# Delta stage of a three-stage decoder layer: pair of batches outside, head groups inside

## The chip, the cores and the metric

The kernel runs on one core of one Trainium2 chip. The metric is the device time of one execution in microseconds (us). Everything is float32.

## The reference

Input x is 8 batches of 256 tokens of width 512. One decoder layer with three parts is computed, and after each part a residual sum and a layer norm over the width (written here with `ln`):

```
x = ln(x + gated_delta_attention(x))   # the stage of this change
x = ln(x + cross_attention(x))         # 32 heads of 16, with a mask
x = ln(x + selected_token_block(x))    # a router picks 1 token of 8, these go through attention and an MLP
```

The first part, per head of 128, with 8 query and key heads and 16 value heads:

```
q, k, v = silu(causal_conv4(x @ w_qkv.T));  q, k = l2_norm(q), l2_norm(k)
beta = sigmoid(x @ w_beta.T);  alpha = exp(-exp(log_A) * softplus(x @ w_alpha.T + dt_bias))
for each token t:                      # S is a 128 x 128 state per value head
    S = S * alpha[t];  u = (v[t] - k[t] @ S) * beta[t];  S = S + outer(k[t], u);  o[t] = q[t] @ S
y = (silu(x @ w_gate.T) * rms_norm(o)) @ w_out.T
```

## The kernel before

`delta_phase` (line 62) does the first part, `cross_phase` (983) the second and `ffn_phase` (1564) the third. Each is a block of five programs, one an engine, written out in full with semaphores between them. The change touches `delta_phase` alone.

The unit of work there is a double: one group of heads (one query and key head with its two value heads; GH = 8 groups) for one pair of batches (2 x 256 = 512 tokens; PAIRS_B = 4 pairs). There are 32 doubles. They are worked through in a software pipeline of slots. Slot w projects double w + 1 (its six products with 128 columns of weights each: query, key, two values, two gates), solves double w (the recurrence within a chunk of 128 tokens, by repeated small products), and finishes double w - 1 (state, output, rms norm, gate, output projection and the sum into `tokens`). `slots` (line 883) calls one function for each engine with w from -1 to 32. Slot -1 only projects, slot 31 has no projection, and slot 32 only finishes double 31.

In the kernel before, double w is group w // 4 and pair w % 4, so four doubles in a row share their weights.

On PE (`pe_slot`, 189) all products of a slot stand in one fixed order: `products`, `turn_tokens`, `post_w0`, then `proj(0)` to `proj(5)` cut in pieces, between which stand the solving steps `f_step(1..4)` and `g_step(1..4)` (64 products of 32 x 32 each), `f32`, `g32`, `f64`, `g64`, and the steps of `post`. `proj(m)` (193) waits for its 128 columns of weights (`w_loaded[m]`), and for the bank that it writes. `post_out` (372) waits for `w_out_loaded` and for `gated_made`.

DVE (`dve_slot`, 625) does the three later taps of the convolution, the scans that make the decays (`scan`, 639), the masks and joins between f and g steps, and the sum into `tokens` (`add`, 679). ACT does the first tap, the activations and some copies out of PSUM. POOL prepares `dec_gam`, `first` and `kq_p`.

SP issues all DMAs of the stage in one queue (lines 890 to 934), in this order: x and the first weights, constants, then, for w from 0 to 31: `rows(w)` (912), three transfers that bring the alphas of double w from a DRAM buffer, spread over all partitions (762 KB; it waits for both scans of double w - 1); at w = 0 also all of `tokens` (4 MB) and four tables; where w is a multiple of 4, six loads of 256 KB into `w_g`, each after the projection m of the double before has read its part (`projected`); and where w % 4 is 1, the 512 KB of `wo_g`, after the last `y_done` of the group before. After the loop come four loads of 1 MB into `x_t`, weights of the second part.

Weights are single-buffered: `w_g` is [128, 4, 6, 128] and `wo_g` is [128, 2, 512].

`decays_from_logits` (684) computes all alphas of all doubles in slot -1. Its last step (718) multiplies by `neg_a` for the two value heads in two instructions. The column order of beta and alpha is that of the doubles (`unit_cols`, 174).

The layer norm of the first part needs all 8 groups of a pair to be added. `average` and `normalise` (727, 735) do it on DVE and `measure` (514) on ACT, for pairs 0, 1 and 2 in slots 30, 31 and 32 (`finished`, 755). That of pair 3 is done at the start of `cross_phase`.

Of the kernel before, what the change touches and what calls it, by code (L numbers as in the profile page):

```python
# [61 lines left out]
def delta_phase(nc, sem_stack, tokens, x_t, ident, sources, alpha_dram, ahead):  # L62

    w_in, conv_w, w_out = sources["w_in"], sources["conv_w"], sources["w_out"]
    with ExitStack() as stack:
# [108 lines left out]
        def unit_cols(tile, c, j):  # L174

            return tile.rearrange("p (g i h j c) -> p i h g j c", g=GH, i=4, h=2, j=VH)[:, :, :, :, j, c]
# [12 lines left out]
        def pe_slot(pe, w, project, solve, post):  # L189
            par, oth, nxt = w % 2, (w + 1) % 2, w + 1  # L190
            batch, group = nxt % PAIRS_B, nxt // PAIRS_B

            def proj(m, k0, k1):
                bank = bank_p[m % 2]
                if k0 == 0:
                    pe.wait_ge(w_loaded[m], 16 * (group + 1))
                    if m < 2:
                        wait(pe, gate_ready, 2 * nxt - 1 + m)
                    else:
                        wait(pe, conv_step, 12 * nxt + 3 * (m - 1))  # L200
                for k in range(k0, k1):
                    mm = pe.matmul(bank[:, :], w_g[:, k, m, :], x_t[:, k, 2 * S * batch:2 * S * (batch + 1)],  # L202
                                   start=(k == 0), stop=(k == KC - 1))
                if k1 == KC:
                    mm.then_inc(projected, 1)
# [166 lines left out]
            def post_out(n):  # L372
                e, c = divmod(n, NC)
                if n == 0:
                    wait(pe, w_out_loaded, 16 * ((w - 1) // PAIRS_B + 1))
                if n < 2:
                    wait(pe, gated_made, 2 * (w - 1) + n + 1)
                for j in range(VH):
                    mm = pe.matmul(y_banks[n][:, :], gated[:, e, j, c * P:(c + 1) * P], wo_g[:, j, :],  # L379
                                   start=(j == 0), stop=(j == VH - 1))  # L380
                mm.then_inc(y_done, 1)
# [106 lines left out]
        def act_slot(act, w, project, solve, post):  # L488
            par, oth, nxt = w % 2, (w + 1) % 2, w + 1
            group = nxt // PAIRS_B  # L490
# [114 lines left out]
            if w - 2 >= DOUBLES - PAIRS_B:  # L605
                measure(w - 2 - DOUBLES + PAIRS_B)
# [18 lines left out]
        def dve_slot(v, w, project, solve, post):  # L625
            par, oth, nxt = w % 2, (w + 1) % 2, w + 1
            group = nxt // PAIRS_B
# [51 lines left out]
            def add(n):  # L679
                at = tokens[:, 4 * ((w - 1) % PAIRS_B) + n, :]  # L680
                wait(v, y_done, 4 * (w - 1) + n + 1)
                v.tensor_tensor(at, at, y_banks[n][:, :], ALU.add).then_inc(y_added, 1)  # L682

            def decays_from_logits():
# [33 lines left out]
                for j in range(VH):  # L718
                    op = v.tensor_tensor(
                        log_alpha.rearrange("p (g b j c) -> p g b j c", g=GH, b=B, j=VH)[:, :, :, j, :],  # L720
                        poly.rearrange("p (g b j c) -> p g b j c", g=GH, b=B, j=VH)[:, :, :, j, :],
                        neg_a[:].rearrange("p (g j o) -> p g j o", j=VH, o=1)[:, :, j:j + 1, :].to_broadcast([P, GH, B, NC]), ALU.mult)
# [32 lines left out]
            finished = w - 2 - DOUBLES + PAIRS_B  # L755
# [132 lines left out]
        with nc.Block() as block:  # L888

            @block.sync  # L890
            def _(sp):
# [26 lines left out]

                for w in range(DOUBLES):
# [5 lines left out]
                    if w and w % PAIRS_B == 0:  # L925
                        for m in range(6):
                            wait(sp, projected, 6 * (w - 1) + m + 1)
                            sp.dma_start(w_g[:, :, m, :], w_in[w // PAIRS_B][:, :, m * P:(m + 1) * P]).then_inc(w_loaded[m], 16)
                    if w % PAIRS_B == 1:
                        wait(sp, y_done, 4 * (w - 1))  # L930
                        sp.dma_start(wo_g[:], w_out[w // PAIRS_B]).then_inc(w_out_loaded, 16)
                sp.wait_ge(projected, 6 * DOUBLES)
                for to, source in ahead[1]:
                    sp.dma_start(to, source).then_inc(ahead[2], 16)

# [1180 lines left out]
```

## Time and profile before

| | us |
|---|---|
| three runs | 2861.43, 2856.67, 2858.89 |
| median | 2858.89 |
| the profiled execution | 2858.66 |
| its span, first to last instruction | 2856.9 |

The page of the profile has busy times of each engine, the span in 40 slices, the DMA queues, the chain that ended last and the costliest groups of instructions. The chain of the page covers only the end of the last stage (from 2629 us on), which says little of the delta stage. In what follows a slot is told by its first `products` matmul (line 228): slot 0 starts at 50.48 us of the span, slot 1 at 91.41, slot 2 at 141.56, slot 6 at 341.78, slot 7 at 393.07, slot 14 at 743.43, slot 22 at 1145.07, slot 30 at 1548.96 and slot 31 at 1599.01; the second part starts at 1673.10.

### The profile page before, as it was taken

The numbers are of one execution on the slowest core, as the hardware profiler recorded it, in microseconds if no ns is written. First come the engines' busy times: TensorE is split into PE (matmuls) and PEld (weight loads), VectorE is DVE, ScalarE is ACT, GpSimd is POOL, SyncE is SP. The second block draws the span as 40 slices with busy tenths as digits, with TensorE's granted clock in tenths as the row PEclk, the third lists the DMA queues.
The fourth block names the chain that finished last, engine by engine and source line by source line (L and its number), as shares of the span: only waits on it lengthen the run. The fifth ranks groups of instructions, "written<-read, shape, count | busy, mean of one in ns | idle before, by whom it ended". The sixth has DMA issues, their size and how long they took to land. (4 is left out here: it accounts for less than half of the span.)

```text
span 2856.9 us, 80959 instructions
## 1 busy us (share of the span) xinstructions
PE 2723.1 (95%) x34198; PEld 1688.1 (59%) x34198; DVE 1829.7 (64%) x5116; ACT 1315.4 (46%) x3201; POOL 548.5 (19%) x690
## 2 busy tenths in 40 slices
PE   6999999999999999999999889999999999986998
PEld 3565655656555565555656556666666666653466
DVE  5565555556556555565656537888888988886533
ACT  3343343434334343343434226666766676774131
POOL 1222212122221222222122132132131221200020
PEclk9999999999999999999999889999999999998999
DMA  5010110110101101101101100000000000001341
GB/s 186 23 36 12 31 46 20 31 29 20 43 17 32 35 13 31 35 13 31 46 2 32 61 31 1 13 7 7 13 1 13 13 2 13 2 1 62 144 185 67
DMA packets 96777, 99.97 MB, mean 35 GB/s; under 512 B 38177, under 2 KB 84385, under 8 KB 95265
## 3 DMA queue, kind: packets, MB, share of 16 engines
q1 hardware_dynamic: 96256, 94.27, 10.3%
q8 instruction: 272, 4.46, 0.7%
q14 instruction: 89, 0.72, 0.1%
q0 software_dynamic: 160, 0.52, 0.0%
HBM read 89.93 MB, written 4.85 MB: 33 GB/s over the span
## 5 line engine op out<-in xcount | busy, mean ns | idle before, releaser
L202 PE MATMUL dr_p<-x_t,dr_w_g 128*128 128x512 f32 x1536 | 742.0, 610 | 11.0 <-DMA dr_w_g<-in_w_in 7.6
L1259 ACT ACTIVATE xa_probs<-xa_probs,xa_low 128x256 f32<-128x256 f32 x1024 | 430.2, 497 | 18.2 <-DVE xa_low L1426 13.8
L202 PEld LDWEIGHTS dr_p<-x_t,dr_w_g 128*128 128x128 f32 x1536 | 268.9, 191 | 227.8 <-issue 217.6
L1191 PEld LDWEIGHTS xa_t<-ident,xa_probs 128*128 128x128 f32 x2048 | 224.6, 141 | 159.3 <-ACT xa_probs L1259 97.8
L1191 PE MATMUL xa_t<-ident,xa_probs 128*128 128x128 f32 x2048 | 286.0, 280 | 21.8 <-ACT xa_probs_t L1265 15.3
L636 DVE SCALAR_TENSOR_TENSOR dr_acc<-dr_p,dr_taps,dr_acc 128x510 f32<-128x510 f32 (+2 forms) x384 | 285.2, 743 | 23.4 <-ACT dr_acc L494 15.5
L1426 DVE CUSTOM_DVE_ANT_0 xa_probs<-xa_s,xa_mask 128x256 f32<-128x256 f32 x512 | 209.6, 409 | 77.5 <-PE xa_s L1178 77.5
L1265 ACT ACTIVATE xa_probs_t<-xa_t 128x512 f32<-128x512 f32 x256 | 152.5, 596 | 230.2 <-PE xa_t L1191 230.2
L1426 DVE CUSTOM_DVE_ANT_0 xa_probs<-xa_s,xa_zeros 128x256 f32<-128x256 f32 x512 | 214.6, 419 | 0.0
L1435 DVE COPY xa_probs_t<-xa_t 128x512 f32<-128x512 f32 x256 | 176.4, 689 | 41.6 <-PE xa_t L1191 30.4
L854 POOL TENSOR_TENSOR dr_first<-dr_n_mat,dr_packed 32x256 f32<-32x256 f32 x128 | 92.1, 719 | 505.1 <-DVE dr_n_mat L762 499.5
L494 ACT ACTIVATE dr_acc<-dr_p,dr_taps 128x512 f32<-128x512 f32 x128 | 87.3, 682 | 181.4 <-PE dr_p L202 181.4
L1178 PE MATMUL xa_s<-xa_keys,xa_q_pair 32*128 32x512 f32 x1024 | 156.2, 651 | 1.7 <-DVE xa_low L1426 1.0
L1206 PEld LDWEIGHTS xa_o<-xa_probs_t,xa_val 128*32 128x32 f32 x4096 | 105.4, 110 | 83.0 <-issue 76.6
L1206 PE MATMUL xa_o<-xa_probs_t,xa_val 128*32 128x128 f32 x4096 | 139.7, 277 | 14.4 <-DVE xa_probs_t L1435 12.8
L868 POOL COPY dr_x_half<-dr_yx 32x256 f32<-32x256 f32 x32 | 12.4, 387 | 729.1 <-DVE dr_yx L677 729.1
L265 PEld LDWEIGHTS dr_g<-dr_yx,dr_f_low 32*32 32x32 f32 x8192 | 83.2, 105 | 110.9 <-issue 63.1
L682 DVE TENSOR_TENSOR tokens<-tokens,dr_m 128x512 f32<-128x512 f32 x64 | 44.0, 688 | 137.8 <-PE dr_m L379 137.8
L379 PE MATMUL dr_m<-dr_wo_g,dr_gated 128*128 128x512 f32 x256 | 126.9, 620 | 0.4 <-DVE dr_gated L832 0.4
L265 PE MATMUL dr_g<-dr_yx,dr_f_low 32*32 32x32 f32 x8192 | 97.8, 195 | 24.1 <-DVE dr_f_low L669 20.5
L255 PEld LDWEIGHTS dr_f<-dr_yx,dr_n_mat 32*32 32x32 f32 x8192 | 82.7, 105 | 64.3 <-DVE dr_yx L770 28.7
L1552 POOL TENSOR_TENSOR xa_by_sin<-xa_raw,sin 128x256 f32<-128x256 f32 x64 | 45.0, 724 | 387.6 <-DVE xa_raw L1303 387.6
(308 smaller groups left out, 4741.3 us busy)
## 6 DMA issues: line engine op xcount, KB each, us to landing
dr_alpha<-alpha_rows SPq DMA_DIRECT2D x64, 254.0 KB
dr_w_g<-in_w_in SPq DMA_DIRECT2D x48, 256.0 KB, 6.0
dr_alpha<-alpha_rows SPq DMA_DIRECT2D x32, 256.0 KB
ff_wide<-in_fw_qkv SPq DMA_DIRECT2D x8, 1024.0 KB, 15.3
x_t<-in_x_t SPq DMA_DIRECT2D x4, 1024.0 KB, 7.3
tokens<-in_x_tok SPq DMA_DIRECT2D x1, 4096.0 KB, 15.7
dr_wo_g<-in_w_out SPq DMA_DIRECT2D x8, 512.0 KB, 3.7
xa_ctx_b<-in_ctx_t SPq DMA_DIRECT2D x8, 512.0 KB, 3.9
```

Of the source, the lines that this page charges most:

```text
L202: mm = pe.matmul(bank[:, :], w_g[:, k, m, :], x_t[:, k, 2 * S * batch:2 * S * (batch + 1)], start=(k == 0), stop=(k == KC - 1))
L265: mm = pe.matmul(bank_g[i, n * TR:(n + 1) * TR], f_low[i, n, :], yx[i, 0, n, :], start=True, stop=True)
L379: mm = pe.matmul(y_banks[n][:, :], gated[:, e, j, c * P:(c + 1) * P], wo_g[:, j, :], start=(j == 0), stop=(j == VH - 1))
L636: v.scalar_tensor_tensor(out=to[:, :, d:S], in0=bank[:, :, 0:S - d], scalar=taps[:, group, m, TAPS - 1 - d:TAPS - d], in1=to[:, :, d:S], o ...
L854: op = g.tensor_tensor(first[i], n_mat[i, :, i], packed[i, LOW:LOW + 1, :].to_broadcast([TR, EA, TR]), ALU.mult)
L1178: pe.matmul(bank_s[i][:, :], q_pair[32 * i:32 * i + 32, par, t, h, q * P:(q + 1) * P], keys[32 * i:32 * i + 32, par, t].rearrange("p k n - ...
L1191: mm = pe.transpose(bank_t[i % 2][:, at:at + P], probs[:, v % 3, i, kind, kt * P:(kt + 1) * P], ident)
L1206: mm = pe.matmul(bank_o[32 * i:32 * i + 32, at:at + P], val[:, par, kind, kt, 4 * t + i, h:h + 2], probs_t[:, v % 2, i, kind, kt, :], star ...
L1259: op = act.activation(at, at, ACT.Exp, bias=low[:, v % 3, i, kind:kind + 1], scale=-1.0)
L1265: act.activation(probs_t[:, v % 2, 2 * m].rearrange("p k t n -> p (k t n)"), bank_t[0][:, :], ACT.Copy)\
L1426: op = dve.tensor_tensor_reduce(out=probs[:, v % 3, i, kind, :], in0=bank_s[i][:, kind * S:(kind + 1) * S], in1=mask[:, par, q, :] if kind ...
L1435: dve.tensor_copy(probs_t[:, v % 2, 2 * m + 1].rearrange("p k t n -> p (k t n)"), bank_t[1][:, :]).then_inc(copied[1], 1)
```

## The change

The doubles are put in another order: double w is now pair w // 8 and group w % 8. All eight groups of a pair of batches follow each other, and then comes the next pair. Four things go with it.

- Each slot needs weights of another group, so SP loads the six parts of `w_g` for every w from 1 to 31 and `wo_g` for every double. The load of `wo_g` for double w - 2 is issued behind the `w_g` loads of w, and the last two stand behind the loop, the first of them ahead of the four 1 MB loads of the second part and the other behind these.
- The columns of beta and alpha take the new order, and the product with `neg_a` is cut in eight instructions where there were two.
- The layer norm of pairs 0, 1 and 2 is done in slots 9, 17 and 25.
- Indices and the values of waits follow.

```diff
@@ -173,7 +173,7 @@
 
         def unit_cols(tile, c, j):
 
-            return tile.rearrange("p (g i h j c) -> p i h g j c", g=GH, i=4, h=2, j=VH)[:, :, :, :, j, c]
+            return tile.rearrange("p (i g h j c) -> p i h g j c", g=GH, i=4, h=2, j=VH)[:, :, :, :, j, c]
 
         EA = 2 * VH * NC
         BLOCK = [slice(TR * i, TR * i + TR) for i in range(4)]
@@ -188,12 +188,12 @@
 
         def pe_slot(pe, w, project, solve, post):
             par, oth, nxt = w % 2, (w + 1) % 2, w + 1
-            batch, group = nxt % PAIRS_B, nxt // PAIRS_B
+            batch = nxt // GH
 
             def proj(m, k0, k1):
                 bank = bank_p[m % 2]
                 if k0 == 0:
-                    pe.wait_ge(w_loaded[m], 16 * (group + 1))
+                    pe.wait_ge(w_loaded[m], 16 * (nxt + 1))
                     if m < 2:
                         wait(pe, gate_ready, 2 * nxt - 1 + m)
                     else:
@@ -372,7 +372,7 @@
             def post_out(n):
                 e, c = divmod(n, NC)
                 if n == 0:
-                    wait(pe, w_out_loaded, 16 * ((w - 1) // PAIRS_B + 1))
+                    wait(pe, w_out_loaded, 16 * w)
                 if n < 2:
                     wait(pe, gated_made, 2 * (w - 1) + n + 1)
                 for j in range(VH):
@@ -487,7 +487,7 @@
 
         def act_slot(act, w, project, solve, post):
             par, oth, nxt = w % 2, (w + 1) % 2, w + 1
-            group = nxt // PAIRS_B
+            group = nxt % GH
 
             def tap(m):
                 wait(act, projected, 6 * nxt + m + 1)
@@ -602,8 +602,8 @@
             if post:
                 wait(act, den_made, w)
                 act.activation(rms_den[:], rms_den[:], ACT.Sqrt).then_inc(rooted, 1)
-            if w - 2 >= DOUBLES - PAIRS_B:
-                measure(w - 2 - DOUBLES + PAIRS_B)
+            if w > GH and w % GH == 1:
+                measure(w // GH - 1)
             if project:
                 silu_v(0)
                 tap(3)
@@ -624,7 +624,7 @@
 
         def dve_slot(v, w, project, solve, post):
             par, oth, nxt = w % 2, (w + 1) % 2, w + 1
-            group = nxt // PAIRS_B
+            group = nxt % GH
 
             def conv(m, first=1, end=TAPS):
                 wait(v, tapped, 4 * nxt + m + 1)
@@ -677,7 +677,7 @@
                 v.transpose(yx[:, 1].rearrange("p n k -> p (n k)"), at).then_inc(yx_done, 1)
 
             def add(n):
-                at = tokens[:, 4 * ((w - 1) % PAIRS_B) + n, :]
+                at = tokens[:, 4 * ((w - 1) // GH) + n, :]
                 wait(v, y_done, 4 * (w - 1) + n + 1)
                 v.tensor_tensor(at, at, y_banks[n][:, :], ALU.add).then_inc(y_added, 1)
 
@@ -715,11 +715,12 @@
                 then(v.tensor_tensor(poly, poly, small, ALU.add))
                 then(v.tensor_tensor(poly, poly, big, ALU.add))
                 v.wait_ge(expa_made, 1)
-                for j in range(VH):
-                    op = v.tensor_tensor(
-                        log_alpha.rearrange("p (g b j c) -> p g b j c", g=GH, b=B, j=VH)[:, :, :, j, :],
-                        poly.rearrange("p (g b j c) -> p g b j c", g=GH, b=B, j=VH)[:, :, :, j, :],
-                        neg_a[:].rearrange("p (g j o) -> p g j o", j=VH, o=1)[:, :, j:j + 1, :].to_broadcast([P, GH, B, NC]), ALU.mult)
+                of_pair = lambda x, i, j: x.rearrange("p (i g b j c) -> p i g b j c", i=4, g=GH, b=2, j=VH)[:, i, :, :, j, :]
+                for i in range(4):
+                    for j in range(VH):
+                        op = v.tensor_tensor(of_pair(log_alpha, i, j), of_pair(poly, i, j),
+                                             neg_a[:].rearrange("p (g j o) -> p g j o", j=VH, o=1)[:, :, j:j + 1, :].to_broadcast([P, GH, 2, NC]),
+                                             ALU.mult)
                 op.then_inc(arg_made, 1)
                 v.wait_ge(alpha_turned, 1)
                 v.tensor_copy(alpha_rows, bank_f[:, 0:2 * P].rearrange("p (a m) -> p a m", a=2)).then_inc(rows_made, 1)
@@ -752,7 +753,7 @@
                 scan(0)
                 scan(1)
                 return
-            finished = w - 2 - DOUBLES + PAIRS_B
+            finished = w // GH - 1 if w % GH == 1 else -1
             if solve:
                 wait(v, kq_done, w + 1)
                 wait(v, dec_gam_made, w + 1)
@@ -916,22 +917,27 @@
                     for at, c, skip in ((1, 0, 1), (P + 1, 1, 1), (S + 1, 1, 0)):
                         sp.dma_start(to[:, :, at:at + P - skip], source[c][:, skip:P].partition_broadcast(P)).then_inc(alpha_loaded, 16)
 
+                def out_weights(w):
+                    wait(sp, y_done, 4 * w)
+                    sp.dma_start(wo_g[:], w_out[w % GH]).then_inc(w_out_loaded, 16)
+
                 for w in range(DOUBLES):
                     rows(w)
                     if w == 0:
                         sp.dma_start(tokens[:], sources["x_tok"]).then_inc(tokens_loaded, 16)
                         for to, source in ahead[0]:
                             sp.dma_start(to, source).then_inc(ahead[2], 16)
-                    if w and w % PAIRS_B == 0:
+                    if w:
                         for m in range(6):
                             wait(sp, projected, 6 * (w - 1) + m + 1)
-                            sp.dma_start(w_g[:, :, m, :], w_in[w // PAIRS_B][:, :, m * P:(m + 1) * P]).then_inc(w_loaded[m], 16)
-                    if w % PAIRS_B == 1:
-                        wait(sp, y_done, 4 * (w - 1))
-                        sp.dma_start(wo_g[:], w_out[w // PAIRS_B]).then_inc(w_out_loaded, 16)
+                            sp.dma_start(w_g[:, :, m, :], w_in[w % GH][:, :, m * P:(m + 1) * P]).then_inc(w_loaded[m], 16)
+                    if w > 1:
+                        out_weights(w - 2)
+                out_weights(DOUBLES - 2)
                 sp.wait_ge(projected, 6 * DOUBLES)
                 for to, source in ahead[1]:
                     sp.dma_start(to, source).then_inc(ahead[2], 16)
+                out_weights(DOUBLES - 1)
 
             @block.tensor
             def _(pe):
```

## Rows read from the trace of the kernel before

**Rows 1.** The page: busy us of each engine; packets and MB of q8.

```profile
PE 2723.1 (95%) x34198; PEld 1688.1 (59%) x34198; DVE 1829.7 (64%) x5116; ACT 1315.4 (46%) x3201; POOL 548.5 (19%) x690
...
q8 instruction: 272, 4.46, 0.7%
```

**Rows 2.** Sums by slot: us, busy of PE, PEld, DVE, ACT, POOL; PE clock, DMA share.

```profile
50.48:91.41 40.93, 37.11 (x702) 19.92 (x700) 22.66 (x41) 13.25 (x22) 12.30 (x17) 0.96 0.32 107
191.63:241.68 50.05, 49.43 (x777) 29.60 (x776) 28.91 (x51) 19.52 (x52) 10.27 (x15) 1.00 0.07 18
341.78:393.07 51.29, 49.63 (x777) 29.69 (x776) 28.90 (x51) 19.52 (x52) 10.27 (x15) 1.00 0.17 48
...
944.87:994.92 50.05, 49.43 (x777) 29.60 (x776) 28.91 (x51) 19.52 (x52) 10.27 (x15) 1.00 0.18 50
1145.07:1198.57 53.50, 51.39 (x778) 30.35 (x777) 28.91 (x51) 19.51 (x52) 10.27 (x15) 0.97 0.16 46
1548.96:1599.01 50.05, 49.43 (x777) 29.60 (x776) 33.54 (x64) 19.71 (x53) 10.27 (x15) 1.00 0.14 55
1599.01:1673.10 74.09, 56.40 (x795) 40.51 (x793) 33.02 (x70) 17.52 (x71) 8.22 (x13) 0.75 0.06 22
```

**Rows 3.** PE at g_step(3), slots 6 and 22; stops of L265; sums of a stretch.

```profile
373.92 0.37 PE L265 MATMUL dr_g<-dr_yx,dr_f_low 32*32 32x32 f32 x19 [1.03 <-issue]
...
1177.52 0.57 PE L265 MATMUL dr_g<-dr_yx,dr_f_low 32*32 32x32 f32 x43 [1.48 <-issue]
...
  issue: 3.6, 3
...
1178.20:1181.60 3.40, 3.40 (x5) 1.34 (x6) 2.89 (x6) 0.23 (x1) 2.20 (x6) 0.51 0.02 5
```

**Rows 4.** DMA queues in 366.5 to 371.2, 371.2 to 372.5, 418.57 to 420.67.

```profile
q1 hardware_dynamic: 2032, 1.01, 76.8%
...
q8 instruction: 1, 0.02, 5.7%
...
q8 instruction: 1, 0.02, 2.8%
```

**Rows 5.** SP's queue in slot 6.

```profile
364.41 2.08 SPq L928 DMA_DIRECT2D dr_w_g<-in_w_in  x3
```

**Rows 6.** DMA issues: count, KB each, median us to landing.

```profile
dr_w_g<-in_w_in SPq DMA_DIRECT2D x48, 256.0 KB, 6.0
tokens<-in_x_tok SPq DMA_DIRECT2D x1, 4096.0 KB, 15.7
```

**Rows 7.** Start of slot 0: DVE, SP, PE, and the landing of wo_g.

```profile
35.87 0.49 DVE L719 TENSOR_TENSOR dr_junk<-dr_junk,dr_neg_a 128x128 f32<-128x128 f32 x2
47.42 3.42 DVE L642 TENSOR_TENSOR_SCAN dr_decay<-dr_alpha,dr_scan_in 128x770 f32<-128x770 f32 x2 [1.92 <-DMA dr_alpha<-alpha_rows]
...
50.87 3.92 SPq L917 DMA_DIRECT2D dr_alpha<-alpha_rows  x3
54.83 2.41 SPq L931 DMA_DIRECT2D dr_wo_g<-in_w_out  x1
...
53.29 4.46 PE L202 MATMUL dr_p<-x_t,dr_w_g 128*128 128x512 f32 x10
58.90 0.75 PE L255 MATMUL dr_f<-dr_yx,dr_n_mat 32*32 32x32 f32 x64 [1.15 <-DVE dr_yx L770]
...
DMA to landing us min/median/max: 7.2/7.2/7.2
```

**Rows 8.** DVE in slots 31 and 32: layer norm, mask(3), add(0).

```profile
1615.92 2.43 DVE L729 BATCH_NORM_STATS2 dr_stats<-tokens 128x6 f32<-128x512 f32 x4
1619.27 0.42 DVE L669 TENSOR_TENSOR dr_f_low<-dr_f,dr_packed 128x256 f32<-128x256 f32 x1 [0.51 <-PE dr_f L255]
...
1663.85 1.91 DVE L741 TENSOR_SCALAR tokens<-tokens,dr_moments,dr_ln_den 128x512 f32<-128x512 f32 x4
1666.76 0.69 DVE L682 TENSOR_TENSOR tokens<-tokens,dr_m 128x512 f32<-128x512 f32 x1 [1.00 <-PE dr_m L379]
```

## The prediction

> **What bounds the kernel now.** I read the page first, then the sums by slot, then the PE instructions of single slots, then the DMA queues. The page [rows 1] shows PE busy for 95% of the span, so time comes only from what makes PE wait. The delta stage runs from 50.48 us (first products of slot 0) to 1673.10, and the sums by slot [rows 2] are nearly constant: a slot takes 50.05 us with 49.43 of PE in it, whether it carries no weights (191.63) or a reload of 1.5 MB (944.87, DMA share 0.18). Of the seven slots that reload weights (2, 6, 10, ... 26) four take 50.05 to 50.07. Two (6 and 14) take 51.29 and one, slot 22, takes 53.50. The last two slots, 31 and 32, have no projection and leave PE gaps.
>
> The three long slots are the clue. In slot 6, PE stops inside the burst of 64 small matmuls of g_step(3), 19 before their end, for 1.03 us, released by "issue", which is by nothing the profile knows [rows 3]. In slot 22 it stops 43 before the end, for 1.48 us. Over the kernel this line has exactly 3 such stops [rows 3]; slot 14 has the third. PE's program is unrolled and comes by a DMA queue of its own, in 272 packets (q8) [rows 1], so one packet per some 250 of its matmuls and weight loads, six a slot. In slot 6 no q8 packet runs from 366.5 to 371.2 us, while the main queue is 77% busy with 2032 packets; the one that PE needs comes after, in 371.2 to 372.5 [rows 4]. PE resumes at 373.92. I read this as an instruction fetch that waited behind the three alpha transfers and the first three weight loads, the latter issued at 22.6 to 24.7 us of the slot [rows 5].
>
> **The change part by part.** The sum is made against the profiled execution's 2858.66 us (span 2856.9), which is 0.23 below the median 2858.89.
>
> *Reordering alone.* The same 32 doubles with the same matmuls are done; PE's instruction count stays, so a fetch falls on the same instruction of each slot as before. Index changes cost 0.
>
> *Steady weight loads.* SP now loads six chunks of w_g in each of slots 0 to 29 and 512 KB of wo_g at each slot's end: 24 x 1.5 + 24 x 0.5 = 48 MB more. A chunk is overwritten when its projection ends and is used a slot (50 us) later; its landing takes 6.0 us [rows 6], and wo_g, loaded at a slot's end for the end of the next, took 7.2 in its slowest place [rows 7], so the weights themselves are on time, by some 40 us. SP waits for projected and y_done, and behind it are only the alpha rows of the next double, which wait for a scan in the middle of the next slot: nothing late. Volume: 2.75 MB a slot against 50 us, at a DMA share of 0.18 as in the reload slots. Cost 0 for data, and 0 is what four of seven reload slots show.
>
> *Fetch stalls in new places.* A quiet slot stalls once it has weights if its fetch is asked for while the burst is queued and is needed in g_step(3), at about 30.9 us of the slot. In quiet slots such a fetch shows itself between 25.5 and 27.6 us: the queue view of that stretch has a q8 packet (slot 7 [rows 4]) or none. I read this stretch for slots 1 to 29: 14 quiet ones have it (1, 4, 5, 7, 12, 13, 15, 19, 20, 21, 23, 27, 28, 29), none of the seven reload slots has it, but the three that stall are those whose fetch came after it. In 4, 12 and 19 the block boundary lies behind the burst by my count of instructions, so these do not stall. In 1 and 23 the fetch is asked for while the burst is still being issued, so I count them half. That is 14 - 3 - 1 = 10 stalls, each at 51.29 - 50.05 = 1.24 us: 12.4 us. Bounds: 0 (four of seven) and 14 x 3.45 = 48.3 if all were as slot 22. I take 12.4, since rows of two equal slots give it.
>
> *Clock.* After the stall of slot 22 PE was granted 0.51 (1.2 GHz) from 1178.20 to 1181.60 [rows 3]; that slot cost 3.45, so 2.2 more than the others. One of three stalls did so. PE had stood for 0.62 and 1.48 us just before. With stalls mostly of 1.03, I take 3 of the 10 new ones: 6.6 us. Bounds 0 and 10 x 2.2 = 22.
>
> The Trainium skill ("Runtime: NRT & Kernel Launch", Instruction fetch mechanics) says that each engine's program is refilled in blocks of 16 KiB by a DMA queue that the sequencer drives, and that this is mostly hidden. The trace agrees with the block size (q8: 272 packets, 4.46 MB) and, in three slots, not with "hidden". A second rule speaks against my reading: "DMA: Bandwidth & Descriptors" (Queues, rings and completion order) says that a DMA engine takes turns between its queues packet by packet, so a fetch would not wait for a queue to drain. Rows 4 disagree. By that rule the two terms above would be 0.
>
> *Slot 0.* Before, slot 0 projects double 1 with weights already there: PE runs proj(0) from 53.29 for 4.46 us, then f_step(1) at 58.90 [rows 7]. Now proj(0) waits for w_g[0] of the next group, which SP issues behind rows(1), which waits for both scans (47.42 to 50.84). SP's three alpha issues take 50.87 to 54.79, because 4 MB of tokens (issued 41.40, 15.7 us to landing [rows 6]) are ahead of them. In this place SP issued wo_g at 54.83 and it landed 7.2 us later, 62.0 [rows 7]. w_g[0] has half its bytes, so I estimate 60.3. The eight small products with neg_a that replace two (0.49 us [rows 7]) cost 0.7 more on the chain to the alpha rows: bounds 0.2 and 8 x 0.245 - 0.49 = 1.5. So proj(0) starts at 61.0, f_step(1) 4.46 later at 65.5, 6.6 us late. The first chunk is not the last wait: w_g[1] follows within some 1.9 us, under the 3.4 us of proj(0). PE, idle for 7.7 us, probably gets the lower clock for a while: 3.4 us at 0.51 cost 1.7; I take 1.4. Together 8.0. Bounds: 5 (load lands with the tokens, no clock loss) and 13 (chunks 1.9 us apart make each projection wait).
>
> *Layer norm of finished pairs.* It moves from slots 30, 31, 32 to 9, 17, 25: 2.43 for the statistics and 1.91 for the normalising [rows 8], some 4.9 us of DVE each with the small steps between. Slot 30 with it took 50.05 as slots without it [rows 2], so 0 in the new places. In slot 31 the statistics end before mask(3), which waits 0.51 us for PE all the same; the normalising delays f_64 (1632.78) by under 1 us, but PE is at post_out(0) from 1631.75 for 3.78. In slot 32 it ends at 1665.76 and add(0) waits 1.00 for PE. Gain 0; bounds 0 and 2 x 4.9 = 9.8.
>
> *Tail.* The 4 MB of cross weights, issued at 1591.07 and landing up to 11 us later, now go behind wo_g of slot 31, at about 1600. They are needed at 1673, but PE's fetch in slot 31, which ran at about 1607.7, would wait until 1612: 0 to 4 us, I take 1.5. The last wo_g is issued at about 1642 and needed at 1663.2: hidden.
>
> Sum: 12.4 + 6.6 + 8.0 + 1.5 = 28.5; 2858.66 + 28.5 = 2887.2.
>
> **The rivals.**
> A: fetches are not held by weight traffic, or only in the phases seen, since the stops of slots 6, 14 and 22 have another cause. For it: four of seven reload slots are clean. Against it: no quiet slot has any such stop. Time: 2858.66 + 8.0 = 2867. (The Trainium skill's rule of queues taking turns, told above, would bring it out this way.)
> B: most stalls take the clock with them and the tail stalls in full: 10 x 3.45 + 2 x 1.24 + 8 + 4 = 49, so 2908. For it: slot 22. Against: slots 6 and 14.
> C: faster. The layer norm on DVE in the drain slots 31 and 32 is what sets mask(3) and the adds; taken away it gives up to 9.8 us, and fetch stalls and slot 0 cost nothing: 2849. It decides from the point where DVE, not PE, ends those waits; the 0.51 and 1.00 us of [rows 8] ended by PE speak against it.
> D: no change. Weights are in time also in slot 0 (the queue drains faster without wo_g there) and fetches as in A: 2859 to 2864. Against it: SP can't issue before 54.8.
>
> **How the numbers follow.** Forecast 0.62, A 0.17, B 0.10, C 0.04, D 0.07. A change under 0.2% (5.7 us) can't be told from none in this kernel. Slower: 0.62 + 0.17 + 0.10 = 0.89, minus 0.01 for a short A: 0.88. Same: D and that 0.01: 0.08. Faster: 0.04. The range takes in A and most of B: 2865 to 2906. The forecast's own terms reach from 2872 (five stalls, no clock) to 2902.
>
> **What would show it.** (1) Slot 0, from its first products to the next, 40.9 us before, is 48 to 50, PE stops before L202 for w_g, 7 to 8 us. (2) L265 has some 13 stops by "issue" in place of 3, each 1 to 1.5 us, in slots 5, 7, 8, 13, 15, 20, 21, 27, 28, 29 and the old ones; slots without them stay at 50.05. (3) The granted clock dips three to four more times between 100 and 1550 us. (4) Slots 9, 17, 25 don't grow by the layer norm, and slots 31 and 32 together stay at 74.1 plus up to 4. If no slot stalls but 6, 14 and 22, the fetch step is wrong; if PE waits for dr_w_g in steady slots, the step on data is.

## The result and the profile after

The changed kernel takes 2881.09 us (median of 6 runs, 2878.95 to 2887.01), the kernel before 2858.28 beside it (6 runs, 2856.67 to 2861.55). The ratio is 1.0084, 95% interval 1.0071 to 1.0096: slower by 22.8 us. The forecast was 2887.2. The profiled execution took 2881.02 us, with a span of 2879.0.

From the page after: busy us and share of the span by engine, the DMA queues, two groups of PE (busy, mean ns | idle before them and its main releaser), and the weight loads with the median us to landing.

```profile
PE 2730.6 (95%) x34198; PEld 1691.2 (59%) x34198; DVE 1829.9 (64%) x5122; ACT 1316.1 (46%) x3201; POOL 548.8 (19%) x690
...
q1 hardware_dynamic: 175744, 144.61, 16.6%
q8 instruction: 272, 4.46, 0.7%
...
L202 PE MATMUL dr_p<-x_t,dr_w_g 128*128 128x512 f32 x1536 | 749.5, 615 | 18.1 <-DMA dr_w_g<-in_w_in 14.8
...
L265 PE MATMUL dr_g<-dr_yx,dr_f_low 32*32 32x32 f32 x8192 | 100.0, 194 | 32.5 <-DVE dr_f_low L669 20.5
...
dr_w_g<-in_w_in SPq DMA_DIRECT2D x192, 256.0 KB, 5.6
```

PE issues the same number of instructions and the same 272 blocks of program as in [rows 1]. The loads of w_g are 192 instead of 48 and land no later than in [rows 6] (median 5.6 us against 6.0). Slots start at other times than before, so the sums are taken from the first `products` of each slot (us; busy of PE, PEld, DVE, ACT, POOL; PE clock, DMA share, GB/s). These are slots 0, 5, 6, 7, 8, 9, 15 and 22, slots 31 and 32 together, and the stretch of low clock in slot 7:

```profile
52.02:100.45 48.43, 38.70 (x701) 20.55 (x700) 22.31 (x40) 13.26 (x22) 10.64 (x16) 0.89 0.44 126
301.65:352.26 50.61, 49.70 (x777) 29.76 (x776) 28.91 (x51) 19.54 (x52) 10.27 (x15) 1.00 0.21 59
352.26:403.40 51.14, 49.63 (x778) 29.68 (x777) 28.91 (x51) 19.54 (x52) 10.28 (x15) 1.00 0.21 58
403.40:456.91 53.51, 51.39 (x778) 30.33 (x777) 28.91 (x51) 19.54 (x52) 10.27 (x15) 0.97 0.23 56
456.91:508.98 52.07, 49.65 (x778) 29.71 (x777) 28.91 (x51) 19.54 (x52) 10.27 (x15) 1.00 0.23 57
508.98:559.03 50.05, 49.42 (x778) 29.60 (x777) 33.52 (x64) 19.74 (x53) 10.26 (x15) 1.00 0.22 60
810.37:863.19 52.82, 51.30 (x778) 30.26 (x777) 28.90 (x51) 19.55 (x52) 10.25 (x15) 0.97 0.22 57
1164.81:1217.92 53.11, 51.32 (x778) 30.12 (x777) 28.92 (x51) 19.54 (x52) 10.29 (x15) 0.97 0.20 56
1620.86:1696.28 75.42, 55.94 (x795) 39.93 (x794) 23.51 (x44) 17.18 (x69) 8.22 (x14) 0.77 0.18 71
436.90:440.31 3.41, 3.41 (x6) 1.35 (x4) 2.54 (x6) 0.00 (x0) 2.44 (x7) 0.50 0.03 5
```

Slots 2 to 4, 9 to 12, 16 to 19, 23 to 26 and 30 take 50.04 to 50.08 us, as the quiet slots of [rows 2] did; slot 9 does so with 4.6 us more of DVE work, the layer norm. The others are longer; those not shown, 1, 13, 14, 20, 21, 27, 28 and 29 take 51.03, 50.53, 50.68, 50.74, 50.67, 50.88, 50.51 and 51.30. The 14 longer slots carry 18.9 us over 50.05, against 5.9 before.

PE's own order in time, in slots 0, 8 and 31 (start, us, count, idle before and its releaser), and the sum of PE's idle time at L265 between 100 and 1615 us, which is slots 1 to 30:

```profile
62.06 7.61 PE L202 MATMUL dr_p<-x_t,dr_w_g 128*128 128x512 f32 x10 [7.06 <-DMA dr_w_g<-in_w_in]
...
487.42 0.31 PE L265 MATMUL dr_g<-dr_yx,dr_f_low 32*32 32x32 f32 x10 [0.62 <-DVE dr_f_low L669]
489.52 0.67 PE L265 MATMUL dr_g<-dr_yx,dr_f_low 32*32 32x32 f32 x54 [1.80 <-issue]
...
1634.73 0.72 PE L255 MATMUL dr_f<-dr_yx,dr_n_mat 32*32 32x32 f32 x60 [1.11 <-issue]
...
1638.48 0.25 PE L265 MATMUL dr_g<-dr_yx,dr_f_low 32*32 32x32 f32 x4 [1.30 <-issue]
```

```profile
its engine sat idle before it (us, times) until:
...
  issue: 10.7, 14
```

There are 14 stops by "issue" where [rows 3] have 3; a fifteenth stop of this line is the one of 1.30 us in slot 31. In slot 8 the burst of 64 is cut after 10; in the other slots the cut lies elsewhere in the same 64.

SP's queue in slots 0 and 8, and the DMA queues in slot 8 (the second fence: from 482.0 to 486.8, and then from 486.8 to 488.2):

```profile
50.23 4.69 SPq L918 DMA_DIRECT2D dr_alpha<-alpha_rows  x3
54.97 6.93 SPq L933 DMA_DIRECT2D dr_w_g<-in_w_in  x6
...
478.03 1.47 SPq L918 DMA_DIRECT2D dr_alpha<-alpha_rows  x3
479.54 7.82 SPq L933 DMA_DIRECT2D dr_w_g<-in_w_in  x4
```

```profile
q1 hardware_dynamic: 2042, 1.01, 87.6%
...
q1 hardware_dynamic: 47, 0.02, 6.9%
q8 instruction: 1, 0.02, 5.0%
```

For 4.8 us no program block comes in while 2042 packets of the main queue do. When these are through, the block arrives (486.8 to 488.2), and PE goes on at 489.52. This is the picture of [rows 4], now in a slot that was quiet before.

### The profile page after: what moved, and what is told of

The parts are those of the page before. It is cut to its first block and busy times, and to the rows that moved or that the text cites. A ratio compares the mean times of both kernels' runs of the same rounds, so it can differ in the third digit from the quotient of the medians.

```text
span 2879.0 us, 81133 instructions
## 1 busy us (share of the span) xinstructions
PE 2730.6 (95%) x34198; PEld 1691.2 (59%) x34198; DVE 1829.9 (64%) x5122; ACT 1316.1 (46%) x3201; POOL 548.8 (19%) x690
## 3 DMA queue, kind: packets, MB, share of 16 engines
q8 instruction: 272, 4.46, 0.7%
## 5 line engine op out<-in xcount | busy, mean ns | idle before, releaser
L202 PE MATMUL dr_p<-x_t,dr_w_g 128*128 128x512 f32 x1536 | 749.5, 615 | 18.1 <-DMA dr_w_g<-in_w_in 14.8
L202 PEld LDWEIGHTS dr_p<-x_t,dr_w_g 128*128 128x128 f32 x1536 | 271.2, 193 | 239.8 <-issue 222.3
L869 POOL COPY dr_x_half<-dr_yx 32x256 f32<-32x256 f32 x32 | 12.4, 387 | 748.1 <-DVE dr_yx L677 748.1
L265 PEld LDWEIGHTS dr_g<-dr_yx,dr_f_low 32*32 32x32 f32 x8192 | 84.1, 105 | 120.6 <-issue 72.1
L265 PE MATMUL dr_g<-dr_yx,dr_f_low 32*32 32x32 f32 x8192 | 100.0, 194 | 32.5 <-DVE dr_f_low L669 20.5
L255 PEld LDWEIGHTS dr_f<-dr_yx,dr_n_mat 32*32 32x32 f32 x8192 | 82.6, 105 | 64.3 <-issue 29.9
```

The source lines that it names most:

```text
L265: mm = pe.matmul(bank_g[i, n * TR:(n + 1) * TR], f_low[i, n, :], yx[i, 0, n, :], start=True, stop=True)
```

## The experiments

The prediction's theory, "order of arrival": a block of PE's program stands behind all data packets issued before it, and PE stops where it runs out of program. No view shows when a block is asked for. The time used here is an estimate: PE passes the place one block (256 of its records) ahead of the stop at 24.6 to 24.9 us of the slot in 11 of the 14 stopping slots, and at 26.1 to 27.3 in slots 5, 20 and 27. Rivals were that the data of the loads is late, that the new order or the layer norm costs, that the clock alone does it, and that fetches and data take turns. Each kernel is compared with the kernel before on its own chip.

**The new order alone.** Against the changed kernel the loads and their waits are the old ones, so most slots use the weights of another group.

```diff
-                    if w:
+                    if w and w % PAIRS_B == 0:
                         for m in range(6):
-                    if w > 1:
-                        out_weights(w - 2)
+                    if w % PAIRS_B == 1:
+                        wait(sp, y_done, 4 * (w - 1))
+                        sp.dma_start(wo_g[:], w_out[w // PAIRS_B]).then_inc(w_out_loaded, 16)
```

> The new order of doubles and its layer norm in slots 9, 17, 25, with weights loaded only in every fourth slot as before (so most slots use weights of another group; every instruction on the compute engines stays). My theory, that the whole cost lies in the added loads (fetches of PE's program held behind them, the first reload in slot 0, the tail): 2858 to 2860 us, stalls by issue in slots 6, 14, 22 alone, slot 0 at 40.9 us. Rival, that order or layer norm cost something of their own: above 2863. Rival, that the layer norm's leaving the drain slots gives something: below 2855.

Measured: 2857.08 us, ratio 1.0004 (0.9994 to 1.0014). Nine of the ten runs took 2854.86 to 2857.57; one took 8264.96, which nothing here explains and which is not in the ratio. Slots 0, 6 and 7, and 31 with 32:

```profile
53.37:93.73 40.36, 37.06 (x701) 19.61 (x700) 22.31 (x40) 13.25 (x22) 11.91 (x17) 0.96 0.32 104
344.17:395.44 51.27, 49.63 (x777) 29.69 (x776) 28.90 (x51) 19.52 (x52) 10.27 (x15) 1.00 0.17 48
395.44:445.50 50.06, 49.44 (x778) 29.60 (x777) 28.89 (x51) 19.52 (x52) 10.27 (x15) 1.00 0.06 18
...
1598.90:1672.29 73.39, 56.23 (x795) 40.34 (x793) 23.59 (x44) 17.15 (x69) 8.20 (x13) 0.77 0.05 22
```

PE stops at L265 in 6, 14 and 22 alone. The order, the layer norm in slots 9, 17 and 25 and the eight small products cost nothing that shows. The last two slots are 0.7 us shorter than before: the most that the layer norm can have given. Even this need not be its work, since the old order mended (below) has 73.12 us there with the layer norm where it was.

**The loads alone.** The kernel before, but w_g and wo_g loaded again in every slot, with the values that they hold already.

```diff
-                    if w and w % PAIRS_B == 0:
+                    if w:
                         for m in range(6):
-                    if w % PAIRS_B == 1:
-                        wait(sp, y_done, 4 * (w - 1))
-                        sp.dma_start(wo_g[:], w_out[w // PAIRS_B]).then_inc(w_out_loaded, 16)
+                    if w > 1:
+                        out_weights(w - 2)
```

> The old order of doubles, with its weights loaded again in every slot (the same values). My theory: the cost comes back in full, 2879 to 2883 us, with stalls by issue in slots 1, 5 to 8, 13 to 15, 20 to 22, 27 to 29, slot 0 near 48. Rival, that the cost comes from the order (which weights or alphas are read when): 2858 to 2862.

Measured: 2878.68 us, ratio 1.0083 (1.0060 to 1.0105). Slots 0 and 20:

```profile
51.50:101.53 50.03, 38.97 (x701) 20.46 (x699) 22.30 (x40) 13.26 (x22) 11.92 (x17) 0.90 0.44 133
1061.58:1114.61 53.03, 51.17 (x777) 30.37 (x776) 28.90 (x51) 19.54 (x52) 10.29 (x15) 0.97 0.20 56
```

Within the interval the loads are the whole loss, though not slot by slot: slot 0 is 1.6 us longer than in the change and slots 1 to 30 are 1.6 us shorter together. Slots 1, 5, 6, 8, 13 to 15, 20 to 22 and 27 to 29 are long; of the 14 only slot 7 is not.

**Fewer packets ahead of the fetch.** The first two loads of w_g go ahead of the alpha rows (their parts are free early in the slot), the other four stay behind.

```diff
                 for w in range(DOUBLES):
+                    if w:
+                        chunks(w, range(2))
                     rows(w)
...
                     if w:
-                        for m in range(6):
-                            wait(sp, projected, 6 * (w - 1) + m + 1)
-                            sp.dma_start(w_g[:, :, m, :], ...).then_inc(w_loaded[m], 16)
+                        chunks(w, range(2, 6))
```

> As the changed kernel, but SP issues the first two weight loads of a slot as soon as their projections end (about 7 and 14 us into the slot), ahead of the alpha rows, so the burst at 21 us of a slot has one weight load in it and not three; the bytes are the same. My theory (a fetch waits for what is queued ahead of it): the burst is drained by about 27 us of the slot, all stalls at g_step(3) vanish, also in 6, 14 and 22, and slot 0 starts a few us earlier: 2856 to 2862 us. Rival, that the stalls come from the amount of traffic in a slot and not its place: within 3 us of 2881.

Measured: 2862.79 us, ratio 1.0022 (1.0013 to 1.0032). Slots 0 and 8, and then the DMA queues of slot 8 from 473.88 to 476.70 and from there to 478.00:

```profile
53.29:98.67 45.38, 37.60 (x701) 20.24 (x699) 22.30 (x40) 13.25 (x22) 11.30 (x17) 0.92 0.48 142
449.28:499.33 50.05, 49.43 (x777) 29.61 (x776) 28.89 (x51) 19.52 (x52) 10.27 (x15) 1.00 0.21 60
```

```profile
q1 hardware_dynamic: 1069, 0.53, 82.5%
...
q1 hardware_dynamic: 163, 0.08, 21.6%
q8 instruction: 1, 0.02, 4.3%
```

The same bytes in each slot, and no stop by "issue" in any of slots 1 to 30. The block still comes after the queue has run down, but from 476.78, 27.5 us into the slot, instead of 29.9. Of the 22.8 us some 6 (by the ratio) to 8 (by the medians on this chip) are left: slot 0 has 5.1 us of wait for w_g left and the last two slots take 75.6.

**The block boundaries moved.** Some small products more in slot -1, before `sums`, shift every later PE instruction against the blocks. One such product in float32 counts as four instruction records. I had taken it for two, so the first kernel, with 64 products, shifts by 256 records (its page has PE and PEld x34326 each, where the change has x34198), a whole block, and not by half of one as its expectation says.

```diff
+                wait(pe, squared, 1)
+                for _ in range(16):          # 8 in the second kernel
+                    for n, i in enumerate(BLOCK):
+                        pe.matmul(bank_m[1][i, 0:TR], ones[:, :], qk_sq[:, n // 2, n % 2, 0:TR], start=True, stop=True)
                 sums()
```

> As the changed kernel, with 64 tiny products more in slot -1 (128 instructions of PE more, about 1 us at most), so that each fetch boundary falls 128 instructions earlier in every slot. My theory: the stalls move to the slots whose boundary now falls into the later part of g_step(3): 2, 3, 4, 9, 10, 11, 16, 17, 18, 19, 24, 25, 26 (12 perhaps), and none stays in 5, 6, 7, 8, 13, 14, 15, 20, 21, 22, 27, 28, 29; total within 6 us of 2881. Rival, that the stalling slots are set by their data or by the order of doubles: the same slots as in the changed kernel stall.

Measured: 2879.45 us, ratio 1.0082 (1.0061 to 1.0102). The stops stay in the same slots, 1, 5, 7, 8, 13 to 15, 20 to 22 and 27 to 29, with slot 6 down to 50.29 and slot 16 at 50.18. The expectation failed, and for the reason above the run tells only that the small products by themselves do nothing. With 32 products it is half a block:

> The run with 64 tiny products moved every PE instruction by 256 records, a whole block of its program, since each product is four records; so it was no shift, and the same slots stalled. Here 32 tiny products stand in slot -1, 128 records, half a block. My theory: the stalls leave 1, 5 to 8, 13 to 15, 20 to 22, 27 to 29 and come in slots 2, 3, 4, 10, 11, 17, 18, 19, 24, 25, 26, with 9, 12 and 16 at the border; the total stays within 6 us of 2881. Rival, that a stalling slot is made by its place in the order or its data: the same slots as before.

Measured: 2877.20 us, ratio 1.0073 (1.0053 to 1.0093). Slots 3, 8 and 18:

```profile
204.03:255.13 51.10, 49.58 (x778) 29.67 (x776) 28.90 (x51) 19.54 (x52) 10.29 (x15) 1.00 0.20 58
456.44:506.49 50.05, 49.43 (x778) 29.59 (x777) 28.90 (x51) 19.54 (x52) 10.29 (x15) 1.00 0.21 60
959.31:1012.29 52.98, 51.37 (x777) 30.17 (x776) 28.90 (x51) 19.54 (x52) 10.27 (x15) 0.97 0.22 56
```

The set turns over. Slots 2, 3, 4, 10, 11, 17, 18 and 24 to 26 now stop at L265, and 6 to 8, 13 to 15, 20 to 22, 28 and 29 are at 50.04 to 50.08. Slot 5, which the expectation had as quiet, stays at 50.53, but its stop (1.02 us) is now at L202; slot 16, at the border, takes 50.31. No data, no wait and no length of a product has changed in them. Counting PE's records from the first, each such stop of slots 1 to 30 falls on the same place of a block of 256 (193 or 194), and so does the one at L202 in slot 5. This holds in each of the six traces counted so (before, the change, the loads alone, the two of this section, and slot 0 alone).

**More packets, ahead and behind.** A spare transfer of 192 KB (384 packets) in each slot, once between the alpha rows and the first load of w_g, once behind the third load.

```diff
+                        wait(sp, spare_loaded, 16 * (w - 1))      # first kernel: ahead of the loop over m
+                        sp.dma_start(spare[:], w_in[w % GH][:, 0:3, 0:P]).then_inc(spare_loaded, 16)
                         for m in range(6):
                             wait(sp, projected, 6 * (w - 1) + m + 1)
                             sp.dma_start(w_g[:, :, m, :], ...).then_inc(w_loaded[m], 16)
+                            if m == 2: ...                        # second kernel: the same two lines here
```

> As the changed kernel, with one more transfer of 192 KB (384 packets) in every slot, into a tile that nobody reads, issued between the alpha rows and the first weight load. My theory, that a fetch waits for all that stands in the queues before it: about 1 us more (384 packets at some 350 in a us) in each of the 14 stalling slots, some new stalls at the borders (4, 12, 19, 23, 30), 2892 to 2905 us. Rival, that a fetch takes turns with the queue: within 3 us of 2881.

> The same 192 KB in each slot, but issued behind the third weight load, at about 25 us of the slot, which is after the critical fetch has been asked for (24.4 to 24.9). If the DMA engines serve in order of arrival, the stalls stay as they are: 2879 to 2885 us. If instead the fetch is served last, when the queue runs dry, they grow as in the run with the transfer ahead: 2892 to 2905.

Measured: 2881.25 us ahead (2875.19 and 2887.31; 1.0087, 1.0058 to 1.0116), 2883.82 behind (1.0096, 1.0076 to 1.0116). Behind came out as expected. Ahead did not: neither the median nor, in the profiled run (2875.19), the stops grew; they are 0.27 to 1.32 us there. SP's queue shows why, in slot 7 of the first kernel, which begins at 404.30:

```profile
426.96 0.51 SPq L934 DMA_DIRECT2D dr_spare<-in_w_in  x1
427.51 2.98 SPq L937 DMA_DIRECT2D dr_w_g<-in_w_in  x3
```

and of the second, beginning at 404.29:

```profile
426.94 2.04 SPq L935 DMA_DIRECT2D dr_w_g<-in_w_in  x3
429.03 2.25 SPq L938 DMA_DIRECT2D dr_spare<-in_w_in  x1
```

Ahead, SP needs until 430.49 for the third load, 26.2 us into the slot and so later than the 24.7 at which the fetch is taken to be asked for; behind, until 428.98. The spare transfer pushed a bigger one past the fetch: 1536 + 384 + 1024 = 2944 packets were ahead of it instead of 3072. That fits the theory, but it was seen only afterwards, and the two runs of each kernel lie too far apart to tell the kernels from each other by time. The run that was built on it:

**The third load behind the fourth.** The fourth waits for a projection that ends later, so this keeps exactly two loads (2560 packets) ahead of the fetch.

```diff
-                        for m in range(6):
+                        for m in (0, 1, 3, 2, 4, 5):
```

> As the changed kernel, but the third weight load is issued behind the fourth, at 30 us of the slot, so 2560 packets and not 3072 stand ahead of the critical fetch (with the extra transfer of 192 KB ahead there were 2944, since it pushed the third load behind the fetch). Arrival order: the fetch starts at 28.0 to 28.8 us of a slot, where it was 28.6 to 29.9 with three loads and 26.9 to 28.3 with one; stalls of 0 to 0.6 us in under ten slots, 2866 to 2873 us. If instead the length of the whole burst, or traffic as such, mattered, the stalls would stay: 2878 or more.

Measured: 2870.56 us, ratio 1.0053 (1.0035 to 1.0071). Slots 5 and 8:

```profile
302.16:356.27 54.11, 51.32 (x778) 30.26 (x776) 28.90 (x51) 19.54 (x52) 10.28 (x15) 0.97 0.20 55
456.77:506.81 50.04, 49.41 (x777) 29.58 (x776) 28.91 (x51) 19.54 (x52) 10.30 (x15) 1.00 0.21 60
```

The time came out as expected, and nearly all slots. Slots 5, 7, 14, 15 and 27 remain longer (54.11, 50.42, 50.64, 50.85, 50.93) and the rest are quiet: 6.8 us in all over 50.05 instead of 18.9. The miss is slot 5, which takes most of that: its block started at 30.8 and PE stopped for 2.17 us, where 28.8 and 0.6 were the most expected.

Four kernels now differ in the packets issued ahead of the fetch. In slots 5, 7, 13, 15, 21, 27 and 29, the mean time of the slot at which the block's packet starts:

| ahead of the fetch | packets | block starts, mean (range) | over 50.05, slots 1 to 30 |
|---|---|---|---|
| alpha rows (kernel before) | 1536 | 26.5 (26.0 to 27.5) | none in these slots |
| and one load (two go before the rows) | 2048 | 27.7 (26.9 to 28.3) | none |
| and two loads (third behind fourth) | 2560 | 28.6 (27.4 to 30.8) | 6.8 |
| and three loads (the change) | 3072 | 29.2 (28.7 to 29.9) | 18.9 |

Each 512 packets put the block off by 0.6 to 1.1 us. With the change PE's last program before it ends at 30.8 to 31.3, and PE resumes 2.5 to 2.8 us after the block's start (slot 8: 29.9 and 32.6), so by this estimate a start before about 28.4 costs nothing.

The traces can also say how many packets went first. In these seven slots the main queue had started 1529, 2055, 2519 and 2955 packets on the mean between 21 us of the slot and the block's start, for the four rows of the table. The two kernels with the spare transfer had 2925 (ahead) and 3107 (behind), with the block at 29.1 and 29.3. Order of arrival gives 2944 and 3072 for them; a block that waited for the whole queue would have let 3456 go first. Single slots differ (2480 to 3420 with the transfer behind).

**Slot 0 alone.** Four of the six loads for double 1 are issued in slot -1, before the alpha rows and the tokens.

```diff
+                for m in range(4):
+                    chunk(1, m)
                 sp.wait_ge(rows_made, 1)
...
-                        for m in range(6):
+                        for m in range(4 if w == 1 else 0, 6):
```

> As the changed kernel, but four of the six weight loads for double 1 are issued in slot -1, as soon as the projections of double 0 have read their parts, ahead of the alpha rows and the tokens. My theory: PE's wait of 7 us before proj(0) of slot 0 goes, slot 0 is back at 41 us, total 7 to 8 us less than 2881, about 2873; all stalls at g_step(4) stay. Rival, that another wait takes its place in slot 0 (the scans and dec_gam come later too, or the tokens behind): 2876 or more.

Measured: 2873.91 us, ratio 1.0062 (1.0045 to 1.0079). Slots 0 and 5:

```profile
53.28:91.81 38.53, 35.45 (x701) 19.42 (x699) 22.31 (x40) 13.26 (x22) 10.85 (x16) 1.00 0.43 127
292.83:346.75 53.92, 51.13 (x777) 30.33 (x776) 28.91 (x51) 19.54 (x52) 10.29 (x15) 0.97 0.20 55
```

Slot 0 has no wait for w_g and is 9.9 us shorter than in the change; the median is 7.2 lower, as the stops of the later slots stay and vary from run to run (slot 5 took 2.16 us and a stretch of low clock here).

**Both cures, in the new and in the old order.** The new order with four early loads for double 1, two loads ahead of the alpha rows later on, and the 4 MB for the second part ahead of the last two wo_g; and the kernel before with two loads ahead of the alpha rows in its seven reload slots, nothing else.

```diff
+                chunks(1, range(4))                        # new order
                 sp.wait_ge(rows_made, 1)
...
+                    if w > 1:                              # old order: if w and w % PAIRS_B == 0
+                        chunks(w, range(2))
                     rows(w)
```

> The new order with the first two weight loads of a slot ahead of the alpha rows, four weight loads of double 1 in slot -1, and the 4 MB of cross weights issued ahead of the last two loads of wo_g, as in the kernel before. My theory: no stall at g_step(4) in any slot (5.9 us of before's own three go too), slot 0 back at 41 us, tail back at 74: 2881.1 - 18.9 - 7.5 - 1.3 = 2853.4 us, ratio about 0.998 to the kernel before. Rival, that steady loads keep a small price (50.07 for 50.05 a slot, scans and fetches shifted): 2856 to 2860, no gain.

> The kernel before with one edit: in the seven slots that reload weights the first two loads are issued ahead of the alpha rows. My theory: the stalls of slots 6, 14 and 22 go, 4 to 6 us less than the kernel before: 2853 us, ratio 0.998. Rival, that they move to other instructions: no change.

Measured: the new order 2851.83 us (11 runs, 2850.20 to 2854.92), ratio 0.9983 (0.9974 to 0.9992); the old order 2852.76 (11 runs, 2851.16 to 2854.91), ratio 0.9988 (0.9979 to 0.9997); the kernel before 2856.61 (21 runs). New order, slots 0 and 5, and 31 with 32:

```profile
54.09:94.96 40.87, 37.09 (x701) 19.77 (x700) 22.31 (x40) 13.26 (x22) 12.33 (x17) 0.96 0.44 134
295.31:346.49 51.18, 49.62 (x777) 29.67 (x776) 28.91 (x51) 19.54 (x52) 10.30 (x15) 1.00 0.22 58
...
1598.02:1670.74 72.72, 55.60 (x795) 39.96 (x793) 23.61 (x44) 17.19 (x69) 8.24 (x14) 0.79 0.10 37
```

Old order, slot 6:

```profile
343.88:393.94 50.06, 49.44 (x777) 29.60 (x776) 28.91 (x51) 19.54 (x52) 10.30 (x15) 1.00 0.18 49
```

Both are faster than the kernel before by less than 0.2%, with intervals that end just below 1, and not to be told from each other (0.9 us apart, intervals overlap). The old order has no stop left in slots 6, 14 and 22. The new order has one, in slot 5, where the block started at 29.7 though only 2048 packets were ahead. The queue moved slowly there: SP's three alpha issues took 2.94 us where slot 8 has 1.47, and 1122 packets had started by 27 us of the slot where slot 8 has 1583. Why is open.

## Why the prediction was right, and what was mis-sized

The direction and the mechanism were right, and the time is 6.1 us under the forecast. By its own steps:

*Reordering, layer norm, small products: 0.* Shown by the run of the order alone (1.0004).

*Data of steady loads: 0.* Right. From slot 0 on, PE waits for w_g in slot 0 alone, and with the same bytes in another order (two loads before the rows) no later slot is longer.

*Fetch stalls, forecast 12.4.* The places were right. The ten slots named (5, 7, 8, 13, 15, 20, 21, 27, 28, 29) all stop, 4, 12 and 19 do not, and of the two counted half, 1 does and 23 does not: 11 new stops where 10 were forecast. For slot 8, which has the longest stop, this was luck: its fetch began at 24.9 us of the slot in the kernel before, ahead of the stretch that was read, so it is not among the 14 slots of the working, and the list of signs names it all the same. The size was not right. The stops by "issue" come to 10.7 us in 14, 0.76 each, from 0.26 to 1.80; the forecast took 1.24 a slot, a stop of 1.03 and what goes with it, from slots 6 and 14. Each costs some 0.2 us beyond its recorded length (slot 6: 51.14 - 50.05 - 0.89). The three old stops also became shorter (0.89, 0.47 and 1.17 us). So the step made 7.1 (10.7 - 3.6) and 2.2 (11 x 0.2), together 9.3.

*Clock, forecast 6.6.* There were three stretches at 0.50 (1.2 GHz), in slots 7, 15 and 22, where one was before: two more, not three. They cost 1.7 to 1.8 each beyond the stop (slot 7: 3.46 - 1.50 - 0.2; slot 22: 3.06 - 1.17 - 0.2), where 2.2 was taken, so 3.5. Together with the stalls this is 12.8, by which slots 1 to 30 grew (1520.4 against 1507.6); the forecast had 19.0. These two terms are the mis-sized part of the sum. Which stop takes the clock with it was not forecast well and is not explained: slot 15 lost it after a stop of 0.89, slot 8 kept it after 1.80.

*Slot 0, forecast 8.0: 7.5.* The wait for w_g was 7.06 (forecast 7 to 8), then PE ran proj(0) at 0.50, in 7.61 us instead of the 4.46 of [rows 7], 3.15 more. Against that stand the wait of 1.15 before f_step(1) and a stretch of low clock of the kernel before at 68.9, some 1.7 us, that both went. The clock's net 1.5 is near the 1.4 taken. Shown to be the loads' place by the run with early loads.

*Tail, forecast 1.5: 1.3* (75.42 against the 74.09 of [rows 2]). As the step expected, PE's fetch came behind the 4 MB: SP issued them at 1621.4 to 1623.3, and from 1622 to 1631 no block arrived while the main queue was 99% busy. PE stops by "issue" for 1.11 us at L255 and again for 1.30 us at L265. These are 2.4 us for a growth of 1.3; what gave the rest back is not shown.

*Not forecast.* Slot 0 begins 1.5 us later (52.02 against 50.48). In the kernels of this study it began between 50.5 and 55.0, 53.4 with the loads of before, so it is not put down to the change. With 12.8 over slots 1 to 30, 7.5, 1.3 and 1.5 the parts make 23.1; the profiled runs differ by 22.4, the medians by 22.8.

One name was wrong: the burst in which PE stops is that of g_step(4), not g_step(3). It has the same line and the right time of the slot, and nothing in the sum depends on it.

Of the rivals, A (no fetch stalls) falls with the moved block boundaries and with the two loads ahead of the alpha rows. B had nearly every new stop take the clock with it; 2 of 11 did. C falls with the order alone (0.7 us at most in the last two slots), D with the wait of 7.06 us in slot 0. The rule of the Trainium skill that was weighed ("DMA: Bandwidth & Descriptors", Queues, rings and completion order: a DMA engine takes turns between its queues packet by packet) would have the block come as soon without the third load as with it. The runs say otherwise: it starts later with each load ahead of it, from 26.5 to 29.2 us.

What stays open: in which part of the DMA path the block waits (the starts fit an order of arrival, but no view shows the path), and what decides the clock. Not tried: larger packets for w_g, which would change the number of packets at the same bytes; the study varied both together.

## What to carry to other kernels

In a fully unrolled kernel a DMA burst can stop an engine that needs none of its data, because its program comes by DMA too and here started later with each load issued before it (26.5 to 29.2 us of the slot): where PE stops by "issue" in the midst of equal instructions, look at the instruction queue in that stretch, and at what was issued just before it. The cure here was to move loads, not to save bytes: issue them early, as soon as the buffer is free, so that few packets stand ahead of the next block. Which passes of a loop stop depends on where the block boundaries fall, so an edit elsewhere can move the loss.

## What was not expected of the hardware

By the estimate above, the block of program is asked for only some 6 us (4 in slots 5 and 27) before PE runs out, while the bytes of a block take 0.9 to 1.4 us to come. A transfer of 384 packets put in front made no stop longer, probably because SP's own issue time (0.51 us for the transfer, 1.70 for the third load behind it) moved a larger one past the request. And in one trace the granted clock fell to 0.50 for 3.4 us after a stop of 0.89 us and stayed at 1.00 after one of 1.80.
